# Four image layers on one core: a second queue for the stores between the layers, and a longer loop body in the first

## The reference

```
x = x + L0(group_norm(x))   # attention over the 3x3 window of each pixel, layer norms, GELU, 1x1 convolution
x = x + L1(group_norm(x))   # gates from 1x1 convolutions, the image's mean and its maximum
x = x + L2(group_norm(x))   # 3x3 window: sum of P/Q, P of degree 5 in the pixel, Q = 1 + |degree 4|
x = x + L3(group_norm(x))   # 3x3 window: B-spline bases and SiLU, weighted

# L1
out1, out3 = mean(x), max(x)
wh   = sigmoid(tanh(W2(Wc x + bc) / (out1 + eps) + b2))
gray = sigmoid(tanh(W3(W1 x + b1) / (out3 + eps) + b3))
out  = W4 (x * (1 + wh + gray)) + b4
```

## Time and profile before

| | us |
|---|---|
| median of 3 runs (9913.86 to 9939.9) | 9925.01 |
| the profiled execution | 9921.5 |
| its span, first to last instruction | 9919.7 |

### The profile page before, as it was taken

One profiled execution on the slowest core, in us unless ns is written; L12 is line 12 of the kernel. 1 busy time (PEld: TensorE's weight loads), 2 busy tenths in 40 slices (PEclk: granted clock), 3 DMA queues, 4 the chain that ended last, 5 costly groups with the idle time before them and its releaser, 6 DMA issues. The chain is left out here.

```text
span 9919.7 us, 141478 instructions
## 1 busy us (share of the span) xinstructions
PE 8149.7 (82%) x35038; PEld 2741.3 (28%) x35038; DVE 7774.4 (78%) x9339; ACT 7513.9 (76%) x8313; POOL 6175.0 (62%) x3353
## 2 busy tenths in 40 slices
PE   6999999999999995306888888888888888883689
PEld 2333333333333331101222222222222222220233
DVE  6777777777777776867888888888888888885777
ACT  4676666666666673557899989989889899893787
POOL 3555555555555552007888888888888888882111
PEclk9999999999999997658999999999999999996899
DMA  2000000000000001253323323223223223235555
GB/s 85 13 12 11 11 13 12 11 11 13 12 11 11 11 9 76 100 181 82 66 55 69 66 55 69 64 57 69 62 60 69 60 61 69 58 62 132 130 137 128
DMA packets 258450, 565.42 MB, mean 57 GB/s; under 512 B 71660, under 2 KB 179788, under 8 KB 244184
## 3 DMA queue, kind: packets, MB, share of 16 engines
q1 hardware_dynamic: 221746, 536.51, 22.2%
q0 software_dynamic: 35744, 17.87, 1.0%
HBM read 367.15 MB, written 186.72 MB: 56 GB/s over the span
## 5 line engine op out<-in xcount | busy, mean ns | idle before, releaser
L1226 POOL TENSOR_TENSOR l_a<-l_a 128x1018 f32<-128x1018 f32 x2116 | 3923.1, 1885 | 581.7 <-ACT l_a L1389 569.5
L1351 DVE TENSOR_TENSOR l_r<-l_pps,l_a 128x509 f32<-128x509 f32 x4232 | 2641.8, 680 | 640.2 <-PE l_pps L1239 640.1
L1389 ACT ACTIVATE l_a<-l_a 128x2036 f32<-128x2036 f32 x1193 | 2269.9, 1903 | 116.3 <-DVE l_a L1357 94.0
L1239 PE MATMUL l_qps<-l_mv,wst 123*128 123x509 bf16 x4246 | 1317.7, 393 | 722.9 <-DMA l_mv<-pw 408.3
L1382 ACT ACTIVATE l_a<-l_qps 128x1018 f32<-128x1018 f32 x1592 | 1592.3, 1019 | 380.0 <-PE l_qps L1239 370.8
L599 POOL TENSOR_TENSOR a_pr<-a_pr 128x768 f32<-128x768 f32 x384 | 896.6, 2335 | 811.1 <-DVE a_pr L537 795.2
L1239 PE MATMUL l_pps<-l_mv,wst 123*128 123x509 bf16 x4232 | 1348.0, 389 | 9.8 <-DVE l_r L1351 1.5
L675 ACT ACTIVATE a_g<-a_fps 128x512 f32<-128x512 f32 x1152 | 645.8, 596 | 757.5 <-PE a_fps L419 632.1
L1292 PE MATMUL l_aux<-l_r,l_sums 128*32 128x509 f32 x8448 | 1131.0, 607 | 51.0 <-DVE l_o L1335 30.2
L1357 DVE TENSOR_SCALAR l_a<-l_qps 128x1018 int32<-128x1018 int32 x796 | 961.0, 1207 | 9.3 <-PE l_qps L1239 8.0
L537 DVE TENSOR_TENSOR a_pr<-a_qkv,a_at 128x768 f32<-128x768 f32 x576 | 854.8, 1537 | 2.2
(11 more groups left out here) (180 smaller groups left out, 11931.8 us busy)
## 6 DMA issues: line engine op xcount, KB each, us to landing
l_mv<-pw SPq DMA_DIRECT2D x1608, 79.5 KB
l_gx<-g SPq DMA_DIRECT2D x66, 1040.0 KB
l_sh<-planes SPq DMA_DIRECT2D x536, 127.2 KB, 6.7
planes<-l_s SPq DMA_DIRECT2D x66, 1018.0 KB, 4.6
a_xt<-g SPq DMA_DIRECT2D x192, 160.0 KB, 3.3
pw<-pw_hi SPq DMA_DIRECT2D x20, 1000.0 KB
pw<-pw_mid SPq DMA_DIRECT2D x20, 1000.0 KB
pw<-pw_lo SPq DMA_DIRECT2D x20, 1000.0 KB
```

The costliest lines, as they stand in the source:

```text
L1226: g.tensor_tensor(a, a, a, ALU.mult).then_inc(sq_p, 1)
L1239: return t.matmul(out, wst[:, k, n * P:(n + 1) * P], x[:, n // NPP, cols], start=True, stop=True)
L1351: v.tensor_tensor(to, pps[:, (2 * m + h) % P_BANKS, 0:SUB], pair_of(A, m)[:, h, :], ALU.mult).then_inc(mul_done, 1)
L1389: s_.activation(a, a, ACT.Abs_reciprocal_sqrt, bias=1.0).then_inc(root_done, GROUP)
```

## The change

- Layer 0's loop has 5 passes of `ROUNDS` = 12 chunks in place of 15 passes of 4.
- norm0: loads and column stores alternate between SP's and ACT's queue.
- Layer 1: x is loaded in two halves of rows, one on SP's and one on ACT's queue, each followed by every other piece of x1. The addition, the statistics and a new maximum per piece walk the image along its rows, in runs of 16 columns; the last maximum is taken over the 1,024 maxima per partition. A buffer of ones is made by POOL and stored to DRAM. Several semaphores are merged or dropped.
- Powers: `hi` of every chunk and `lo` of odd chunks are stored by SP, `mid` of every chunk and `lo` of even chunks by POOL. Chunk k waits for both queues' stores of chunk k - 3.
- Layer 2: the rows of ones are loaded from DRAM behind each of the first three supertiles' loads; DVE's three fills are gone; the constants are loaded behind the first supertile; PE waits at its start for all five of these small transfers.
- Layer 3, first block: out2's pieces come on ACT's queue with five slots, x2's on SP's, the weights after all of x2 and their preparation at piece 6; the stores of g3 are split in halves between SP and ACT.

```diff
@@ layer 0
-    with engine.Fori(0, (LEAD_OUT - LEAD_IN) // TURNS) as thrice:
-        for i in range(TURNS):
-            body(Plan(thrice * TURNS + (LEAD_IN + i), (LEAD_IN + i) % TURNS, LEAD_IN))
+    with engine.Fori(0, (LEAD_OUT - LEAD_IN) // ROUNDS) as again:
+        for i in range(ROUNDS):
+            body(Plan(again * ROUNDS + (LEAD_IN + i), (LEAD_IN + i) % TURNS, LEAD_IN))
@@ norm0
+                for k in (0, 2):
+                    load(sp, k)
+                for k in range(0, W // COLS, 2):
+                    store(sp, k)
...
+                for k in (1, 3):
+                    load(act, k)
                 norm.scalar_part(act)
+                for k in range(1, W // COLS, 2):
+                    store(act, k)
@@ layer 1
+            def load(e, half):
+                rows = slice(half * HW // 2, (half + 1) * HW // 2)
+                e.dma_start(X[:, rows], x[:, rows]).then_inc(x_in[0], 16)
+                for k in range(half, LOADS, 2):
+                    n = HW // LOADS
+                    e.dma_start(G[:, k * n:(k + 1) * n], x1[:, k * n:(k + 1) * n]).then_inc(x_in[k], 16)
...
-                    image, laid = X[:].rearrange("p (h w) -> p w h", w=W), G.rearrange("p (w h) -> p w h", h=H)
+                    image, laid = X[:].rearrange("p (h w) -> p h w", w=W), G.rearrange("p (w h) -> p h w", h=H)
...
+                            e.wait_ge(x_in[j], 16 if j else 64)
+                            link(v.scalar_tensor_tensor(image[:, :, at], laid[:, :, at], shift0[:], image[:, :, at], ALU.add, ALU.add))
+                            v.tensor_reduce(tops[:, j, :], image[:, :, at], AX.X, ALU.max)
...
-                    link(v.reduce_max(top[:, 0:1], X[:], AX.X))
+                    link(v.reduce_max(top[:, 0:1], tops[:].rearrange("p k h -> p (k h)"), AX.X))
@@ powers
             @block.sync
+                    sp.wait_ge(hi_ready, (k + 1) * DEG)
+                    sp.dma_start(lines[0, :, :, :, at:at + n], hi[:, k % BUF, :, 0:n]).then_inc(stored[k % BUF], 16)
+                    if k % 2:
+                        sp.wait_ge(lo_ready, (k + 1) * DEG)
+                        sp.dma_start(lines[2, :, :, :, at:at + n], lo[:, k % BUF, :, 0:n]).then_inc(stored[k % BUF], 16)
...
+            @block.gpsimd
+                    pool.wait_ge(mid_ready, (k + 1) * DEG)
+                    nc.gpsimd.dma_start(lines[1, :, :, :, at:at + n], mid[:, k % BUF, :, 0:n]).then_inc(stored_p[k % BUF], 16)
+                    if k % 2 == 0:
+                        pool.wait_ge(lo_ready, (k + 1) * DEG)
+                        nc.gpsimd.dma_start(lines[2, :, :, :, at:at + n], lo[:, k % BUF, :, 0:n]).then_inc(stored_p[k % BUF], 16)
@@ layer 2
                 for g in range(SLOTS):
-                    sp.wait_ge(mv_cleared, g + 1)
                     load_supertile(g, g)
+                    sp.dma_start(mv[KROWS - 3:KROWS, g].rearrange("p c n -> p (c n)"), ones).then_inc(c_in, 16)
+                    if g == 0:
+                        sp.dma_start(sums[:], l2w[0]).then_inc(c_in, 16)
+                        sp.dma_start(pick[:], l2w[1]).then_inc(c_in, 16)
...
-                pe.wait_ge(c_in, 32)
+                pe.wait_ge(c_in, 80)
...
-                for u in range(SLOTS):
-                    v.memset(mv[:, u], 1.0).then_inc(mv_cleared, 1)
@@ layer 3
-            Y = sb1("l3_y", [P, 3, ROWS * PW])
+            Y = sb1("l3_y", [P, YSLOTS, ROWS * PW])
...
-                        if p == 3:
+                        if p == 6:
                             e.wait_ge(w_in, 7 * 16)
...
+                    for k in range(PIECES):
+                        if k >= YSLOTS:
+                            act.wait_ge(added, k - YSLOTS + 1)
+                        at = PW + k * ROWS * PW
+                        rows = out2[:, LEAD:].rearrange("c (b n) -> b c n", b=NB)[:, :, at:at + ROWS * PW]
+                        act.dma_start(Y[:, k % YSLOTS, :], rows).then_inc(x_in[k], 16)
                     norm.scalar_part(act)
+                    store(act, 1)
```

More of the change, by code:

```diff
@@ L156 @@
 LEAD_IN, LEAD_OUT = 3, NCHUNKS - 1
[L157 removed]
+assert FS == 64 and 2 * HREST == P and SETS * FS == P and ROUNDS % TURNS == 0 and (LEAD_OUT - LEAD_IN) % ROUNDS == 0
 class Plan:
@@ L204, in norm0, with load, store @@
         chain, ready, edges, stored = sem("n0_chain"), sem("n0_ready"), sem("n0_edges"), sem("n0_stored")
+        def load(e, k):
+            e.dma_start(X[:, k * HW // 4:(k + 1) * HW // 4], x[:, k * HW // 4:(k + 1) * HW // 4]).then_inc(x_in[k], 16)
+        def store(e, k):
+            cols = slice(1 + k * COLS, 1 + (k + 1) * COLS)
+            e.wait_ge(ready, 3 * (k + 1))
+            e.dma_start(g0[:, cols, :], G[:, cols, :]).then_inc(stored, 16)
         with nc.Block() as block:
@@ L717, in _, with layer1 @@
                 steps(act, body)
-def layer1(nc, x, x1, bias0, x2, pair, w1, raw2, pieces, wst, pw):
+def layer1(nc, x, x1, bias0, x2, pair, w1, raw2, pieces, ones, wst, pw):
     TILE = 1024
@@ L747, in layer1 @@
             top = sb1("l1_top", [P, 8])
+            tops = sb1("l1_tops", [P, LOADS, H])
+            one = sb1("l1_one", [ONES, SUB], BF16)
             stat = sb1("l1_stat", [P, 8])
@@ L784, in _ @@
                     sp.dma_start(rest2[:], raw2).then_inc(raw_in, 16)
[L785 to L790, removed]
+                    sp.dma_start(shift0[:], bias0).then_inc(x_in[0], 16)
+                    load(sp, 0)
                     norm.sync_part(sp, pair)
@@ L798, in _ @@
                         sp.dma_start(flat, part2[:, m, :]).then_inc(stored, 16)
+                    sp.wait_ge(one_made, 1)
+                    sp.dma_start(ones.rearrange("r n -> (r n)").rearrange("(p n) -> p n", p=ONES), one[:]).then_inc(stored, 16)
                     for k in range(4):
@@ L922, in _ @@
                     s = nc.scalar
+                    load(act, 1)
                     norm.scalar_part(act)
@@ L970, in powers, with by_sp, by_pool, wait_stored @@
         stored = [sem(f"pw_stored{u}") for u in range(BUF)]
+        stored_p = [sem(f"pw_stored_p{u}") for u in range(BUF)]
+        def by_sp(k):
+            return sum(1 + j % 2 for j in range(k % BUF, k + 1, BUF)) * 16
+        def by_pool(k):
+            return sum(2 - j % 2 for j in range(k % BUF, k + 1, BUF)) * 16
+        def wait_stored(e, k):
+            e.wait_ge(stored[k % BUF], by_sp(k))
+            e.wait_ge(stored_p[k % BUF], by_pool(k))
+        lines = pw.rearrange("t c i (b n) -> t b c i n", b=NB)
         def power(k, i):
@@ L1468, in layer3, with store @@
             zeroed, g_ready, g_stored = sem("l3_zeroed"), sem("l3_g_ready"), sem("l3_g_stored")
+            def store(e, half):
+                for k in range(PIECES):
+                    e.wait_ge(g_ready, k + 1)
+                    lo = k * ROWS // CROWS
+                    hi = lo + ROWS // CROWS if k < PIECES - 1 else NCK
+                    for j in range(half * QUAD // 2, (half + 1) * QUAD // 2):
+                        to = g3[lo:hi, :, :, j, :].rearrange("k e c n -> (e c) k n")
+                        src = G[32 * j:32 * j + 32, lo * CROWS:hi * CROWS, :].rearrange("p (k r) w -> p k (r w)", r=CROWS)
+                        e.dma_start(to, src).then_inc(g_stored, 16)
             with nc.Block() as block:
@@ L1784, in build @@
     pw = dram("pw", (3, C, DEG, LINE), BF16)
+    ones = dram("ones", (3, NCG * SUP), BF16)
     pieces = dram("pieces", (3, CG * DEG + 1, 2 * WCOLS), BF16)
```

92 lines of the change are left out of this document (33 added, 59 removed).

## The result

The changed kernel took 9864.8 us (median of 4 runs, 9853.2 to 9880.9), the kernel before, on the same chip, 9932.5 (4 runs, 9913.9 to 9944.8): a ratio of 0.9935, 95% interval 0.9912 to 0.9957. That is 68 us less, where 128.5 were forecast. The kernel became faster, and most of the gain lies in the two stages that the forecast named first, but it is half of what I had worked out.

What follows compares the result with a forecast made beforehand. It took no stage as transfer-bound while multiplying, powers as bound by its stores, and priced the seams and layer 0's turns: -45 - 90 - 17 + 2.5 + 17.5 + 4.5 - 1 = -128.5, from 9925.0 to 9797 us; 8-in-10 range 9745 to 9890.

Steps and rivals of the forecast that it cites:

- the two stages that the forecast named first: Layer 0's loop, forecast at -45 us, and powers, forecast at -90 us.
- powers' term: Powers' stores: split evenly over SP and POOL, the busy half holds 47 stores, pace 12.7 us a chunk, -90 us.
- the start of layer 2: Layer 2's start: TensorE waits for ones behind 72 loads, starting 42.5 us after SP, +17.5 us.
- layer 1: Layer 1: cheaper addition, statistics and last maximum on VectorE, -17 us; shared engines for loads, +2.5 us.
- layer 3's first block: Layer 3's start: same bytes and engines, weights' sum moved to piece 6, -1 us (-8 to +6).
- Layer 0: Layer 0's loop: 4 turns instead of 14 at a fixed 4.5 us each, -45 us (0 to -63).
- The term "+2.5": Layer 1's load: x1's first piece, 1.05 MB at 421 GB/s, shares the engines with the second input, +2.5 us.
- norm0: norm0's loads: on two queues the first and second quarters arrive together, when the second did, +4.5 us (0 to 4.9).
- The second queue gives nothing: Rival for powers: stores share the same engines, pace stays at 17 us a chunk, kernel 9887 us; chance 0.11.
- A turn's price grows with its body: Rival for layer 0's loop: longer turns cost more, so layer 0 gives nothing, kernel 9842 us; chance 0.09.
- POOL sets the pace: Rival for powers: POOL's stores hold it back and the kernel is slower, 9971 us at 14 us a store; chance 0.06.
- VectorE sets powers' pace: Rival for powers: the second queue overlaps fully, 10.95 us a chunk, 36 us more gain, kernel 9761 us; chance 0.20.

Runs made afterwards that it cites:

- fixed split: Changed kernel with SP storing the high part of every powers chunk, GpSimd the middle and low parts: 9837.5 us (one run).
- kernel with one queue: Changed kernel with norm0's, layer 1's and layer 3's first-block loads and stores all back on SP, none on ScalarE's queue: 9892.7 us, ratio 0.9970.
- the two kernels with 60 and 20 chunks: Changed kernel, powers' stores all on GpSimd, ones first, ScalarE's queue given back, old layer 3, 60 or 20 chunks per layer 0 turn: 9737.1, 9765.8 us.
- the kernel with the ones first: Changed kernel with layer 2's rows of ones and two small tables issued before the supertile loads: 9821.9 us, ratio 0.9891.

## Why the gain was half of the forecast

**The step that failed** is the size of powers' term: "the busy half holds 31 + 16 = 47 stores instead of 63, a pace of 12.7 us", hence -90. It measured -51, and these 39 us are most of what is missing from the 128.5; the start of layer 2 misses 8.7, layer 1 8.5, layer 3's first block 7. The mechanism stands: a store on SP's queue fills half of the engines (53%), ScalarE's queue fills the same half, GpSimd's fills both. What was wrong is the price of a store on the shared half: I gave every one SP's own 5.65 us, and took for granted that two queues get as much out of these engines as one. The rows give the rates. SP alone brings 181 GB/s through its half. GpSimd alone brings 241 through both, at 86.2% busy, so 140 through a full half. Where both meet, if GpSimd's stores fall evenly on both halves, the half of SP carries its own 1.5 stores and half of GpSimd's 1.5, 2.3 MB in 14.7 us, 157 GB/s; with the fixed split 1 and half of 2, 2.05 MB in 14.8 us, 138 GB/s. That is the measured pace turned round: it gives the size of the slip, about -47 us (21 chunks of 2.25) in place of -90, and no reason for it. No row of the kernel before had both queues on one half, so the price could only be guessed there. GpSimd's packets take more engine time for a MB: 43.7% of 16 engines over 170 us for 17.86 MB are 67 us for each MB, against 50 for SP's in the same stretch and 57 for GpSimd's when it is alone. A part of that is waiting: with half of GpSimd's time on it, SP's half would be busy 110%.

SP's queue is what is late, not GpSimd's: one store in 9.8 us in the changed kernel, one in 13.6 with the fixed split. By the Trainium skill (DMA: Bandwidth & Descriptors, "Queues, rings and completion order") an engine takes packets from its queues in turn. An estimate by that: SP's packets took 79 ns (33.3% of 16 engines, 170 us, 11510 packets) and GpSimd's 150; a store of SP has some 81 packets on each of 8 engines, 6.4 us by itself and 18.5 if one of GpSimd's goes between each two. The measured 9.8 and 13.6 lie between, the higher one where GpSimd has more to send. Which packets stood in whose way was not tried further.

**Layer 0, right, and in part by luck.** A turn costs 3.9 to 4.6 us with 12 chunks (15.5 to 18.5 for four, in nine profiles), and two turns fewer with 20 gave 8.9. The price is no constant: single turns cost 2 to 7 us, and fourteen of them 63.3 us in one execution of the kernel before and 50.6 in the other. Against the second the gain is 33 us and not 48.

**Layer 1: VectorE right, the load wrong.** The term "+2.5" counted one more piece of x1. The queue does not stop after one piece: it had brought 3.55 MB of x1 by the time of the first addition, which came 8.9 us later. The kernel with one queue shows the two parts apart: -16.5 us against before without the second queue, and 10.5 of them lost again with it. (The same code gave 219.8 us in place of 217.7 in the two kernels with 60 and 20 chunks.)

**Start of layer 2: the wait right, the rate wrong.** "These are 5.86 MB, and the queue moved 6.83 MB in 44 us here": that stretch held a store of long rows beside the loads, and while it ran the rate was twice as high (293 and 315 GB/s). Up to 4529, with loads alone, the kernel before moved 3.83 MB in 28 us, 137 GB/s where I took 155: by that the loads need 42.8 us and not 37.8. In the changed kernel they ran at 128 GB/s (3.89 MB from 4392.6 to 4423), 45.8 us, an estimate that with my 2 and 1 to 3 for the ends gives 49 to 51 against the measured 51.2. My own terms, 37.8, 2 and 1 to 3, made 40.8 to 42.8, of which I had taken the top. The order was the cost, as the kernel with the ones first shows: -27 us.

**norm0, right** (+4.6 for +4.5): VectorE's first statistics start at 12.90 instead of 8.03.

**Layer 3: not settled.** The first addition is 5 us later with two queues, but the block of the same code differs by 10 us and more between executions (143.7 to 157.2 with one queue), and so does the loop. VectorE waits 54.4 to 67.6 us for out2 in the block with one queue as before, 62.9 to 68.5 with two.

**The rivals.** "The second queue gives nothing" is true of ScalarE's and false of GpSimd's. "A turn's price grows with its body" is false up to 20 chunks. "POOL sets the pace" is false: 1.21 us an issue, against my 0.67 to 6.7. "VectorE sets powers' pace" comes nearest with all stores on GpSimd, 11.5 to 12.2 us against its 10.95.

## What to carry to other kernels

Ask of a second queue which engines it reaches, not how many queues there are: a queue whose steady share stands at 53% tells that half is idle, and only a queue that reaches the other half helps. Here it was best to give it everything, since of two queues on shared engines the later one set the pace. Ahead of a first operation, every load on a second queue that is not needed yet takes bandwidth from the one that is. And what TensorE waits for first must be issued first, however small it is.

## What I had not expected of the hardware

- **A stage that no edit touches can change by 30 us.** The rest of layer 2, the same instructions, took 4511.5 to 4529.8 us in twelve profiles and 4549.0 and 4554.9 in two. These two kernels have other code ahead of it, as most of the twelve have, and both show TensorE's waits for ScalarE at some 70 us instead of 46. Each was profiled once, so it is not known whether the kernel or the execution makes it. I had offered the place of ScalarE's instructions as a cause; two further kernels with other places were at the usual value, which fits it and does not show it. It stays open. It is the largest part of what hid the gain of the kernel with one queue at the seams, 4.8 us in norm0 and 10.5 in layer 1: its 24.9 us there are more than both.
- **Executions differ by stage.** Layer 3's loop does the same work in 734.7 us at a mean granted clock of 0.92 and in 773.2 at 0.90. TensorE's own busy time, 623.0 and 631.6 us, makes 8.6 of the 38.5, and where the rest comes from stays open. Windows of the kernel with the high part on SP and of the one with 20 chunks:

```profile
9100.90:9835.60 734.70, 623.01 (x3664) 225.67 (x3664) 571.47 (x329) 586.68 (x397) 131.20 (x196) 0.92 0.54 132
```

```profile
9007.40:9780.60 773.20, 631.61 (x3664) 228.68 (x3664) 572.02 (x329) 587.68 (x397) 129.98 (x196) 0.90 0.53 126
```

- **Without any turn, each step of layer 0 is 0.45 us shorter** (57.06 against 57.51, alike in all 57), which no row had suggested. What makes them shorter was not tried further.
- **Powers keeps its time on SP's queue alone, and not where GpSimd's has a part.** All stores on SP's queue gave 376.2 us in three profiles; the split of the change 320.0 to 334.9 in five, all on GpSimd's 260.7 to 277.0 in four.
